# Banded attention on one core: GpSimd zeroes the out-of-band probabilities of the second pair of heads, in place of a mask matmul on TensorE

## What is computed

```python
    scores = jnp.einsum('bhid,bhjd->bhij', q, k) * SCALE
    i = jnp.arange(s)[:, None]
    j = jnp.arange(s)[None, :]
    valid = (j <= i) & (j >= i - W + 1)          # W = 32
    scores = jnp.where(valid, scores, -jnp.inf)
    attn = jax.nn.softmax(scores, axis=-1)
    out = jnp.einsum('bhij,bhjd->bhid', attn, v)
```

## Time and profile before

| | |
|---|---|
| median of 3 runs | 1278.41 us (1278.14 to 1282.47) |
| the profiled execution | 1279.5 us, its span 1277.7 us |
| busy, share of the span | PE 1064.8 us (83%), DVE 1051.1 us (82%), ACT 719.0 us (56%), POOL 401.5 us (31%) |
| banded attention, first mask matmul to the end of the last `weigh` | 840.42 to 949.8 us of the span |
| exponentials of the banded attention (line 689) | 128, busy 49.0 us |
| score reductions on VectorE (line 712) | 256, busy 74.4 us |

### The profile page before, as it was taken

The page is one execution under the profiler, slowest core; times in us unless marked ns, Lnnn a source line. Parts: engine busy times, 40 slices in busy tenths (PEclk is TensorE's granted clock), DMA queues, the critical chain, the costliest instruction groups (busy, mean ns, idle before and its releaser), DMA issues. The chain is left out here.

```text
span 1277.7 us, 21430 instructions
## 1 busy us (share of the span) xinstructions
PE 1064.8 (83%) x6168; PEld 435.2 (34%) x6168; DVE 1051.1 (82%) x2149; ACT 719.0 (56%) x1102; POOL 401.5 (31%) x312
## 2 busy tenths in 40 slices
PE   4599989899998553899999996478884599999997
PEld 2112222222221142444444443223344244444443
DVE  6798999889999867688888886577638788888886
ACT  3106777677878612566666664335543366666665
POOL 1000000000000302467677772000001277667675
PEclk9658999889999875899999997679887799999999
DMA  2800110110002820566776660521100286667663
GB/s 68 250 3 26 27 27 2 27 27 6 22 2 92 248 65 0 132 162 160 165 164 158 156 157 0 149 52 53 52 2 19 57 179 160 156 156 160 161 163 95
DMA packets 53394, 120.20 MB, mean 94 GB/s; under 512 B 10296, under 2 KB 36792, under 8 KB 45128
## 3 DMA queue, kind: packets, MB, share of 16 engines
q1 hardware_dynamic: 53320, 119.28, 37.8%
HBM read 103.94 MB, written 14.91 MB: 93 GB/s over the span
## 5 line engine op out<-in xcount | busy, mean ns | idle before, releaser
L476 DVE TENSOR_REDUCE Aatt_mx<-Aatt_sc 128x1 f32<-128x512 f32 x512 | 317.6, 684 | 26.1 <-PE Aatt_sc L352 25.8
L436 ACT ACTIVATE Aatt_prob<-Aatt_st 128x1024 f32<-128x1024 f32 x256 | 247.4, 1023 | 76.6 <-PE Aatt_st L361 75.6
L1385 POOL TENSOR_TENSOR M1ex_low<-M1ex_hid,M1ex_high 128x512 f16<-128x512 f32 x132 | 181.4, 1390 | 92.1 <-ACT M1ex_high L1317 90.3
L1385 POOL TENSOR_TENSOR M2ex_low<-M2ex_hid,M2ex_high 128x512 f16<-128x512 f32 x132 | 181.2, 1389 | 91.5 <-ACT M2ex_high L1317 89.7
L352 PE MATMUL Aatt_sc<-ks,qs 48*128 48x512 bf16 x512 | 176.5, 431 | 28.9 <-DVE Aatt_mx L476 7.2
L372 PE MATMUL Aatt_pv<-Aatt_prob,vg 128*32 128x512 f32 x1024 | 142.0, 628 | 1.0 <-ACT Aatt_prob L436 0.6
L1356 DVE TENSOR_TENSOR M2ex_hid<-M2ex_act_up,M2ex_cb 128x512 f32<-128x512 f32 x132 | 138.1, 1046 | 3.7 <-DMA M2ex_cb<-comb 3.7
L1356 DVE TENSOR_TENSOR M1ex_hid<-M1ex_act_up,M1ex_cb 128x512 f32<-128x512 f32 x132 | 137.8, 1045 | 3.9 <-DMA M1ex_cb<-comb 3.7
L1347 DVE SCALAR_TENSOR_TENSOR M1ex_act_up<-M1ex_up,unscale,M1ex_sil 128x512 f32<-128x512 f32 x132 | 98.5, 746 | 36.2 <-ACT M1ex_sil L1312 32.6
L1347 DVE SCALAR_TENSOR_TENSOR M2ex_act_up<-M2ex_up,unscale,M2ex_sil 128x512 f32<-128x512 f32 x132 | 98.5, 746 | 35.5 <-ACT M2ex_sil L1312 33.4
L1312 ACT ACTIVATE M1ex_sil<-M1ex_gate,unscale 128x512 f32<-128x512 f32 x132 | 90.7, 687 | 63.9 <-PE M1ex_gate L1265 60.2
(11 more groups left out here) (270 smaller groups left out, 1804.0 us busy)
## 6 DMA issues: line engine op xcount, KB each, us to landing
M1ex_cb<-comb SPq DMA_DIRECT2D x64, 512.0 KB, 6.6
M2ex_cb<-comb SPq DMA_DIRECT2D x64, 512.0 KB, 6.6
M_wt<-wsplit SPq DMA_DIRECT2D x66, 192.0 KB
wsplit<-split_cut SPq DMA_DIRECT2D x9, 704.0 KB, 6.9
split_raw<-in_wg_dram SPq DMA_DIRECT2D x6, 704.0 KB, 5.2
stack<-Aqkv_part SPq DMA_DIRECT2D x16, 192.0 KB, 3.2
qs<-stack SPq DMA_DIRECT2D x32, 96.0 KB
ks<-stack SPq DMA_DIRECT2D x32, 96.0 KB
```

What stands on the lines that cost most here:

```text
L436: act.activation(prob[e % 4][:, :, :].rearrange("p a c -> p (a c)"), st[pr][:, :, :].rearrange("p a c -> p (a c)"), ACT.Exp, scale=SCALE). ...
L476: dve.tensor_reduce(mx[k][:, m, part // 2:part // 2 + 1], sc_bank(k, i)[:, :], AX.X, ALU.max).then_inc(red_done, 1)
L1385: pool.tensor_tensor(low[i % 3][:, :], hid[i % 3][:, :], high[i % 3][:, :], ALU.subtract).then_inc(low_ready, 1)
```

## The change

For pair 0 nothing changes. For pair 1 the mask matmul is gone: the first score matmul of each head starts the bank anew, the exponential is taken of all columns, and GpSimd then writes zeros into the probability tile outside the band, with two affine selects in place: `below` over columns 0 to 127 of both heads, and `above` over columns 32 to 159 (32 to 127 in step 7). The second waits for the first, and `weigh` waits for the second. In a stage GpSimd first does `copy_v` and then the eight `clear`s.

```diff
@@ attend_banded, gpsimd
+            def clear(n, s):
+                e = n * 2 * STEPS + 2 * s + 1
+                by_head = prob[e % 4][:, :].rearrange("p (h r) -> p h r", h=2)
+                end = BAND if s < STEPS - 1 else P
+                pool.wait_ge(exp_done, FREE_ST + e + 1)
+                below = by_head[:, :, 0:P]
+                pool.affine_select(out=below, in_=below, compare_op=ALU.is_ge, fill=0.0, base=0,
+                                   pattern=[[0, 2], [1, P]], channel_multiplier=-1).then_inc(cleared, 1)
+                pool.wait_ge(cleared, e)
+                above = by_head[:, :, WIN:end]
+                pool.affine_select(out=above, in_=above, compare_op=ALU.is_ge, fill=0.0, base=-1,
+                                   pattern=[[0, 2], [-1, end - WIN]], channel_multiplier=1).then_inc(cleared, 1)
...
                     copy_v(n + 1, (k + 1) % 3)
+                for s in range(STEPS):
+                    clear(n, s)
@@ attend_banded, tensor
                 pe.wait_ge(exp_done, FREE_ST + n * 2 * STEPS + 2 * s + 2)
+                pe.wait_ge(cleared, n * 2 * STEPS + 2 * s + 2)
...
                         pe.wait_ge(exp_done, n * 2 * STEPS + e + 1)
-                        pe.matmul(bank[:, :], env.ident16[:, :], mask_k[:, :], start=True, stop=True)
+                        if pr == 0:
+                            pe.matmul(bank[:, :], env.ident16[:, :], mask_k[:, :], start=True, stop=True)
...
-                                           qs[k][rows, h, s * P:s * P + width], start=False, stop=True,
+                                           qs[k][rows, h, s * P:s * P + width], start=pr == 1, stop=True,
```

More of the change, by code:

```diff
@@ L532, in attend_banded @@
         (v_ready, sc_done, red_done, m_step, turned, m_copied, max_ready,
-         st_done, exp_done, pv_done, u_out) = map(sem, (
+         st_done, exp_done, cleared, pv_done, u_out) = map(sem, (
             "v_ready", "sc_done", "red_done", "m_step", "turned", "m_copied",
-            "max_ready", "st_done", "exp_done", "pv_done", "u_out"))
+            "max_ready", "st_done", "exp_done", "cleared", "pv_done", "u_out"))
         block = ctx.enter_context(nc.Block())
```

## The result

The changed kernel takes 1295.1 us (median of 4 runs, 1291.4 to 1298.3), the one before 1278.3 (4 runs, 1277.0 to 1282.5). The ratio is 1.0121, with a 95% interval of 1.0094 to 1.0149: **slower by 1.2%**, 16.8 us, against a forecast of 3.8 us and outside the stated range.

The account below looks back on a forecast made before the run. VectorE's ring of four reductions and one hand-over, not TensorE, was taken to bound the banded part; 1.05 - 0.15 - 1.8 + 0 + 2.7 + 1.0 + 1.0 = +3.8 us, forecast 1282.2 us, range 1277 to 1292.

Parts of the forecast that it names:

- Clock: ... I take one more fall, about +1.0: Banded part: longer hand-over pauses and less TensorE work a step cause one more fall of the clock, about +1.0 us.
- Stages 0 and 4: Stages beginning at 1.2 GHz: faster steps without one mask matmul, less the longer hand-over, -0.9 us each, -1.8 in all.
- the 2.0 I had put down for `cut_max` and one fall: Banded part: `cut_max` waits for selects, 0.15 us a stage, seven times, +1.0; one more clock fall, about +1.0.
- clock rival: Hand-overs: the clock falls at most of them, five stages at about +0.9 us, stage 7 wholly at 1.2 GHz; 1287; chance 0.13.
- slow-select rival: GpSimd's clear: selects of 0.54 us or more bound every step; at 0.6 us 1290, at 0.75 about 1302; chance 0.17.
- From the exponential to `weigh(7)`: Clear at a stage's end: 0.08 + 0.41 + 0.14 + 0.41 + 0.05 = 1.09 us, where 0.05 stood before.
- The DMA wait at the hand-overs: Hand-overs of stages 1, 2 and 5: TensorE's wait for the maxima's DMAs would be gone, the DMA chain no longer deciding.
- The ring of stage 7: Stage 7: exponential, clear, `weigh` and scores set all eight steps, 1.45 us each; at 1.2 GHz about 3.5 for two.
- The reductions were not slowed: Rival on VectorE: GpSimd holds up the reductions, a step gains 0.4 us or more, above 1300; chance 0.05.
- The middle of a stage at full clock: Steps in mid-stage: the clear is covered, cost 0; steps still 1.58 us apart, TensorE's wait in the scores at 0.3 us.
- the rival that TensorE was the bound: Banded part: removing 64 masks at 0.15 us, and 0.26 in some ten slow steps, gives 10.5 us: 1268, faster; chance 0.04.
- 0.7 more for a slow stretch: Stage 7: the same stretch at 1.2 GHz as before adds 0.29 us a step, +0.7, on top of 13.0.

Follow-up runs that it names:

- the changed version that held the clock for a while: The changed kernel with pair 1's mask matmul kept in stage 0 only and idle matmuls filling the waits for the clear in all stages: 1288.04 us, ratio 1.0058.
- The filled version with mask and clear: The changed kernel with pair 1's mask matmul put back and idle matmuls in `weigh` ahead of its wait for the clear: 1281.57 us, ratio 1.0016.
- the change with a risen clock: The changed kernel with pair 1's mask matmul kept and the wait for the clear filled with idle matmuls in stage 0 only: 1289.8 us, ratio 1.0078.

## Why the prediction was wrong

**The failed step** is the clock, in two of its places. The step "Clock: ... I take one more fall, about +1.0", and the step "Stages 0 and 4", which took for granted that the clock rises within stage 0 as it did before. It never rose: 0.50 in all eight stages. I had read a fall as the work of one long pause, and looked for pauses of 1.4 us. The trace of before could not show what the rise depends on, and the experiments do: in this loop, on pair 1's mask matmul (the version without the clear), and, once the clock is up, on that matmul and on pauses of 0.9 us alike.

In the terms of the sum: the forecast had stages 1, 2 and 5 at 13.75, stage 3 at 14.22, stages 0 and 4 at 14.26, stage 6 at 13.53 and stage 7 at 13.7. They came to 15.67, 15.65, 15.68, 15.67 and 15.10. That is 5.75 + 1.43 + 2.83 + 2.14 + 1.40 = 13.55 us over, less the 2.0 I had put down for `cut_max` and one fall: 11.55, all of the 11.6 us that the banded part is over its forecast. The rest between 15.4 in one profile and 16.8 in the medians is variation among executions that these profiles do not place.

The **clock rival** named the right cost, half of its mechanism and too small a size. It had the clock fall at most hand-overs, at 0.9 us for each of five stages, 1287 in all. That is what the version with mask and clear does; in the change itself the clock never rose, a stage wholly at 1.2 GHz costs 1.8 us more, and all eight were. Its chance of 0.13 rested on the two falls at long pauses; 0.15 us less of TensorE's work in a step, the half that the change's own clock hung on, was named and given no price of its own.

How the loss divides, by the banded parts of the profiles: 109.36 to 115.40 for the missing mask matmul alone (+6.0: a gain of TensorE's work lost to a clock that stays down), and 115.40 to 124.77 for the clear on top of that (+9.4: 1.08 at each of seven hand-overs, 7.6, and 3.1 in stage 7, less 1.3, because stages 5 and 6 of the version without the clear are 15.46 and 14.96, not 14.58).

**What held.** A select of 256 elements takes 0.407 us (forecast 0.41, within 0.29 to 0.75), so the slow-select rival is out. The Trainium skill (GPSIMD Engine Reference, performance pitfalls) had led to an estimate of 0.6 us by its slower figure; the measured selects side with the slope of the earlier trace rows. From the exponential to `weigh(7)` it is 1.04 us (1.09), though two terms of that sum were off and made up for each other: 0.06 + 0.41 + 0.07 + 0.35 + 0.15, where TensorE began 0.15 us after the select's end and not 0.05, and the step's second select is the smaller one. The DMA wait at the hand-overs is gone. The ring of stage 7 at 1.2 GHz takes 959.39 - 955.92 = 3.47 us for two steps ("about 3.5"):

```profile
955.92 0.45 PE L667 MATMUL Batt_st<-mask,ident 128*128 128x320 bf16 x1
...
957.94 0.45 PE L667 MATMUL Batt_st<-mask,ident 128*128 128x320 bf16 x1
...
959.39 0.45 PE L667 MATMUL Batt_st<-mask,ident 128*128 128x320 bf16 x1
```

The reductions were not slowed (74.2 us against 74.4, median 363 ns), so that rival is out too. The middle of a stage at full clock came as forecast, in the changed version that held the clock for a while: steps of 1.58 us and a wait of 0.31 us in the scores. So the rival that TensorE was the bound is out as well, and the 0.15 us a step are worth nothing there. At 1.2 GHz TensorE is the bound, and a step takes 1.72 us where it took 1.98 with both masks, the 0.26 us forecast.

**What agrees by luck.** The filled version with mask and clear is 3.5 us longer than before, close to the forecast of 3.8, but it is not the changed kernel and gets there by other terms. Its undisturbed stages are 13.85 to 13.87 against 13.75; the 0.10 is near the 0.15 a stage put down for `cut_max`, but whether it is that was not tried. The rest differs both ways. Its stage 0, with both mask matmuls, is 15.48 and not 14.26, and its stage 6 is 14.15 and not 13.53. Its stage 7, at full clock throughout, is 13.57, where the forecast had 13.0 and 0.7 more for a slow stretch. Its stage 4 is 13.85 and not 14.26, and the 1.0 us for one more fall is not there.

**Open.** What it is about that matmul that counts. It is the one of the step that covers 128*128 of the array by its row, the others have 51*128, 48*128 and 128*32; no version replaced it by as long a matmul of another form. That its result is not what counts is shown: in the version with mask and clear GpSimd writes the zeros anyway, and the clock rises. But in all versions without it pair 1's score matmuls start the bank anew instead of adding to it, and the two were never taken apart.

## What to carry to other kernels

Work that is taken off TensorE can cost more than it frees: here the second mask matmul of a step, 0.15 us, was hidden behind VectorE, and without it the engine ran eight stages at 1.2 GHz. Before pricing such a change at zero, look in the stretches of the trace for where the clock rises and what TensorE does there, and price the case that it does not: the difference of a slow and a full stage, times all the stages behind the same loop. A busy share near 1 is no sign of safety, since at 1.2 GHz the same work fills more time. Where a pause can't be removed, matmuls whose result nobody reads are a cheap test of whether the clock is what it costs. And compare versions in the same state of the clock: the clear seems to cost 3.5 us beside a kernel that had falls of its own, and costs 6.5 beside one that had none.

## What the hardware showed that was not expected

- A loop with TensorE busy for 14.33 of 14.58 us a stage stayed at 1.2 GHz for 115 us; the same loop with one more matmul of 128x320 a step rose in its first stage. The Trainium skill (TensorE: Matmul & The Clock Gate, "HAM oscillation — how this bites in real kernels") lays a clock that comes and goes to an engine that waits between its bursts. The version with mask and clear agrees in kind, 0.76 to 0.79 in stages 2 to 6 with open pauses and 1.00 with filled ones, though its waits are of 0.9 us and those of the page's kernel of 3 to 5; the version without the clear, low with 0.25 us of idle time a stage, does not.
- In the change with a risen clock the fall came 4 us after the hand-over. TensorE was busy for 0.96 and 1.27 of 1.50 us in the two pieces ahead of it, at full clock, and for 1.49 in the piece of the fall, of which the larger part is already at 1.2 GHz. Its longest wait between the hand-over and the fall was 0.33 us.
- Three idle matmuls after each score tile ahead of stage 0 left stage 0 at 0.72, as without them; a fourth one after group 1's tiles gave 1.00 (13.55 and 13.59 us in two versions). Why so little decides was not looked into.
- Selects on GpSimd with fp32 data of 256 elements take 406 to 416 ns. With the 292 ns of 128 elements that is 0.9 ns an element beyond a fixed part of some 0.18 us. The first `CAST` of `cut_max` took 0.27 instead of 0.18 us in each stage, with a select running beside it, and was the only operation of the banded part on VectorE to lengthen in that trace.
